# A two-layer graph network on one core: row factors of the first head broadcast by TensorE, maxima subtracted between the first steps, first pair of the second layer tile by tile

## The reference

```python
def _L0_gnn_ref(input_features, adj, W, b):
    A = (adj != 0).astype(input_features.dtype)
    hidden = input_features @ W + b
    deg = jnp.sum(A, axis=0)
    return A @ hidden / deg[:, None]

def _L1_gnn_ref(h, adj_mat, W, a):          # 4 heads of 512, SLOPE 0.01
    ht = (h @ W).reshape(N, N_HEADS, N_HIDDEN).transpose(1, 0, 2)
    src = jnp.einsum('hnd,hd->hn', ht, a_src)
    dst = jnp.einsum('hnd,hd->hn', ht, a_dst)
    e = jax.nn.leaky_relu(src[:, :, None] + dst[:, None, :], SLOPE) + adj_mat[None]
    att = jax.nn.softmax(e, axis=-1)
    h_prime = jnp.einsum('hij,hjd->hid', att, ht)
    return h_prime.mean(axis=0)
```

## Time and profile before

| | us |
|---|---|
| median of 3 runs | 2495.39 |
| lowest, highest | 2494.52, 2496.39 |
| the profiled execution | 2494.08 |
| its span | 2492.3 |
| PE busy in it | 2447.1 (98%) |
| DVE busy | 1866.4 (75%) |
| ACT busy | 1258.9 (51%) |
| POOL busy | 49.3 (2%) |

### The profile page before, as it was taken

How to read it: one execution, slowest core, us unless ns; L and a number is a source line. 1 busy time by engine, 2 the same in 40 slices (tenths; PEclk the granted TensorE clock), 3 DMA queues, 4 the chain that set the end, 5 groups by cost and what they waited for, 6 DMA issues and landing times.

```text
span 2492.3 us, 42728 instructions
## 1 busy us (share of the span) xinstructions
PE 2447.1 (98%) x12328; PEld 1198.3 (48%) x12328; DVE 1866.4 (75%) x2560; ACT 1258.9 (51%) x1883; POOL 49.3 (2%) x44
## 2 busy tenths in 40 slices
PE   6999999799999999999999999999999999999999
PEld 3544447344444444444444444444444444444787
DVE  7588767876688766877668776687766887667776
ACT  4545546744455444554445544455444554444554
POOL 0000000000000000000000000000000000000000
PEclk9999999899999999999999999999999999999999
DMA  4286646200030000300003000030000300001000
GB/s 148 69 290 195 227 156 217 82 5 5 25 97 34 4 4 25 97 34 4 4 25 97 34 4 4 25 97 34 4 4 25 97 34 2 2 13 49 26 1 9
DMA packets 74223, 144.21 MB, mean 58 GB/s; under 512 B 4489, under 2 KB 11915, under 8 KB 72970
## 3 DMA queue, kind: packets, MB, share of 16 engines
q1 hardware_dynamic: 74122, 143.08, 17.5%
HBM read 129.37 MB, written 13.70 MB: 57 GB/s over the span
## 4 chain that ended last, share of the span: by engine, by line
PE 94%; DVE 3%; DMA 1%; issue 1%; ACT 1%; SPq 0%; DVEq 0%; ACTq 0%
PE z_ps L731 70%; PE o_ps L759 11%; PE o_ps L1351 3%; PE z_ps L1351 3%; PE z_ps L1404 2%; PE c_ps L1322 1%; PE o_ps L1322 1%; DMA ring_reg<-adjT_in 1%; PE c_ps L1351 1%; DVE hl_reg L917 1%; PE c_ps L1383 1%; PE o_ps L1375 0%; PE o_ps L1309 0%; DMA h_reg<-x_in 0%; DVE w_reg L952 0%
## 5 line engine op out<-in xcount | busy, mean ns | idle before, releaser
L731 PE MATMUL z_ps<-hl_reg,h_reg 128*128 (+2 forms) x8736 | 1759.0, 364 | 11.1 <-DVE hl_reg L608 11.1
L731 PEld LDWEIGHTS z_ps<-hl_reg,h_reg 128*128 (+1 forms) x8736 | 855.2, 98 | 911.4 <-DVE hl_reg L608 11.4
L559 ACT ACTIVATE hl_reg<-t_reg (+2 forms) x364 | 361.9, 994 | 731.5 <-DVE t_reg L635 379.4
L608 DVE TENSOR_TENSOR hl_reg<-t_reg,hl_reg (+2 forms) x364 | 417.6, 1147 | 235.0 <-ACT hl_reg L559 233.3
L544 ACT ACTIVATE t_reg<-ring_reg,vv 128x512 f32 (+3 forms) x728 | 526.3, 770 | 66.0 <-DVE ao_reg L623 60.3
L635 DVE SCALAR_TENSOR_TENSOR t_reg<-t_reg,vv,e_reg (+3 forms) x728 | 510.3, 743 | 7.7 <-issue 7.7
L623 DVE TENSOR_TENSOR ao_reg<-ao_reg,t_reg 128x1024 f32<-128x1024 f32 (+1 forms) x336 | 383.7, 1142 | 0.0
L759 PE MATMUL o_ps<-w_reg,z_reg 128*128 128x512 f16 x1248 | 278.2, 379 | 0.9 <-DVE z_reg L651 0.9
L759 PEld LDWEIGHTS o_ps<-w_reg,z_reg 128*128 128x128 f16 x1248 | 119.8, 98 | 140.9 <-DVE z_reg L651 1.2
L651 DVE SCALAR_TENSOR_TENSOR z_reg<-z_ps,z_reg 128x512 f16<-128x512 f32 (+1 forms) x112 | 73.2, 653 | 151.6 <-ACT z_reg L571 151.6
L456 ACT ACTIVATE e_reg<-e_reg (+2 forms) x91 | 90.1, 996 | 152.0 <-DVE e_reg L467 151.9
(11 more groups left out here) (165 smaller groups left out, 1066.9 us busy)
## 6 DMA issues: line engine op xcount, KB each, us to landing
ring_reg<-adjT_in SPq DMA_DIRECT2D x78, 512.0 KB, 4.6
e_reg<-adjT_in SPq DMA_DIRECT2D x78, 512.0 KB, 3.6
ring_reg<-x_in SPq DMA_DIRECT2D x13, 512.0 KB, 4.2
x_dram<-ring_reg SPq DMA_DIRECT2D x13, 512.0 KB, 5.1
ring_reg<-c_dram SPq DMA_DIRECT2D x24, 256.0 KB, 3.3
ao_reg<-x_dram SPq DMA_DIRECT2D x6, 1024.0 KB, 5.6
out_dram<-ao_reg SPq DMA_DIRECT2D x6, 1024.0 KB, 4.4
h_reg<-x_in SPq DMA_DIRECT2D x3, 1536.0 KB, 16.7
```

Of the source, the lines that this page charges most:

```text
L559: nc.scalar.activation(hl_ring[:, g % HL_RING, 0, :, 0:W], t_ring[:, g % T_RING, :, 0:W], ACT.Copy).then_inc(hi_ready, 1)
L608: nc.vector.tensor_tensor(hl_ring[:, g % HL_RING, 1, :, 0:W], t_ring[:, g % T_RING, :, 0:W], hl_ring[:, g % HL_RING, 0, :, 0:W], ALU.subtr ...
L731: mm = nc.tensor.matmul(z_ps[:, k, 0:W], hk[hs], hl_ring[:, r, ps, u, 0:W], start=first and u == 0 and n == 0, stop=last and u == 1 and n ...
```

## The change

The work is the same but for where scales are applied; the order around the start of the second layer is another.

- **Scores read where they are.** The scaled copy of the scores (L1134) goes; the reduction and the two operations after it read the scores from PSUM, and the factor 1/HS moves into the scale of the exponentials. The exponentials of the column factors go to a buffer of their own (`ev`), from which two DVE operations make the three parts of `vv`; the mask of the last tile follows later, during the first step.
- **Row factors of the first head.** PE makes the broadcast rows itself, by four transpositions of a column of `rows_c` read 128 times over, into one bank; ACT copies the bank to `c_bc[:, 0]`. The rows of all heads are still transposed, copied (from a different buffer) and sent through DRAM, later, and only the heads 1 to 3 are loaded back for block 0.
- **Order on ACT and DVE.** The third early exponential stands behind that of the row factors. The subtractions of the pairs 3, 4 and 5 follow the steps 1, 2 and 3, that of pair 6 and both splits follow step 4; the exponentials of these pairs and the high halves accordingly on ACT.
- **First pair tile by tile.** For pair 0 of segment (0, 0) the high and the low half are made for each tile of 512 columns, and PE takes the first tile (12 matmuls over the four banks) when its low half is there, then the second.

```diff
@@ layer2_scalar(act, c_rows, high1)
                 if isinstance(p, int) and p == 0:
-                    act.wait_ge(c_in[h], (b + 1) * 16)
+                    if isinstance(b, int) and b == 0 and h == 0:
+                        act.wait_ge(c0_sb, 1)
+                        act.wait_ge(s_vvp, 2)
+                    else:
+                        act.wait_ge(c_in[h], (b + (h > 0)) * 16)
...
                 for p in range(2, LOOP0):
                     step(b, h, p)
+                    if isinstance(b, int) and b == 0 and h == 0:
+                        exp_e(act, 0, E_PRE0 + p - 1)
+                if isinstance(b, int) and b == 0 and h == 0:
+                    for j in range(LATE_SPLIT, PAIRS):
+                        high1(j)
...
             t1(0, 0, 0)
-            for p in range(2):
-                step(0, 0, p)
+            for u in range(2):
+                act.wait_ge(p_ready, u + 1)
+                nc.scalar.activation(hl_ring[:, 0, 0, u], t_ring[:, 0, u],
+                                     ACT.Copy).then_inc(f_hi if u == 0 else hi_ready, 1)
+            t1(0, 0, 1)
+            step(0, 0, 1)
+            exp_e(act, 0, E_PRE0)
+            c_rows()
@@ layer2_vector(dve, split1)
                 for p in range(4, LOOP0):
                     step(b, h, p)
+                    if isinstance(b, int) and b == 0 and h == 0:
+                        subtract_max(dve, 0, E_PRE - 1)
+                        for j in range(LATE_SPLIT, PAIRS):
+                            split1(j)
...
-            for p in range(4):
-                step(0, 0, p)
+            step(0, 0, 0)
+            for u in range(2):
+                if u == 0:
+                    dve.wait_ge(f_hi, 1)
+                else:
+                    dve.wait_ge(hi_ready, 1)
+                nc.vector.tensor_tensor(hl_ring[:, 0, 1, u], t_ring[:, 0, u], hl_ring[:, 0, 0, u],
+                                        ALU.subtract).then_inc(f_lo if u == 0 else lo_ready, 1)
+            last = vv[:].rearrange("p (r t) -> p r t", t=NT)[:, :, NT - 1]
+            nc.vector.tensor_scalar(last, last, valid[:, NT - 1:NT], None, ALU.mult).then_inc(s_vmask, 1)
+            accumulate(0, 0, 0)
+            for p in range(1, 4):
+                step(0, 0, p, before=(0, 0, p - 1) if p > 1 else None, lone=p == 1)
+                subtract_max(dve, 0, E_PRE0 + p - 1)
@@ layer2_tensor
-            pair(0, 0, 0, first=True)
+            for u in range(2):
+                if u == 0:
+                    pe.wait_ge(f_lo, 1)
+                else:
+                    pe.wait_ge(lo_ready, 1)
+                for k in range(KT):
+                    for n, (hs, ps) in enumerate(((0, 0), (0, 1), (1, 0))):
+                        mm = nc.tensor.matmul(z_ps[:, k], h16[:, u, hs, k * P:(k + 1) * P], hl_ring[:, 0, ps, u],
+                                              start=u == 0 and n == 0, stop=False)
+            mm.then_inc(hl_free, 1)
@@ sync
                 sp.wait_ge(cr_out, 16)
-                for h in range(H):
+                for h in range(1, H):
                     load_c(sp, 0, h)
@@ vector
                 dve.wait_ge(sd_ps, NT)
-                link(dve, nc.vector.tensor_scalar(sdc, c_ps[:, 0:NT * 2 * H], 1.0 / HS, None, ALU.mult))
-                nc.vector.tensor_reduce(dmx[:], sdc.rearrange("p (t r) -> p r t", r=2 * H), AX_X,
-                                        ALU.max).then_inc(s_dmx, 1)
+                nc.vector.tensor_reduce(dmx[:], sd_rt, AX_X, ALU.max).then_inc(s_dmx, 1)
...
                 dve.wait_ge(s_vv, 2)
...
-                for p in range(E_PRE0, E_PRE):
-                    subtract_max(dve, 0, p)
-                for j in range(LATE_SPLIT, PAIRS):
-                    split1(j)
-                layer2_vector(dve)
+                nc.vector.tensor_scalar(vv4[:, 2], ev4[:, 0], -PS, None, ALU.mult).then_inc(s_vvp, 1)
+                nc.vector.tensor_scalar(vv[:, 0:2 * H * NT], ev, PS, None, ALU.mult).then_inc(s_vvp, 1)
+                dve.wait_ge(s_vvp, 2)
+                layer2_vector(dve, split1)
@@ scalar
-                for p in range(E_PRE0):
+                for p in range(E_PRE0 - 1):
                     exp_e(act, 0, p)
...
+                nc.scalar.activation(cc3, cc3, ACT.Exp, scale=1.0 / HS).then_inc(s_cexp, 1)
+                exp_e(act, 0, E_PRE0 - 1)
+                act.wait_ge(cb_ps, 1)
+                act.wait_ge(x1_out[0], 16 * sum((NA + i) % ADJ_RING == 0 for i in range(PAIRS)))
+                nc.scalar.activation(c_bc[:, 0], o_ps[:, 1], ACT.Copy).then_inc(c0_sb, 1)
@@ tensor
                 pe.wait_ge(tr_sb, NT)
+                for t in range(IT):
+                    mm = nc.tensor.transpose(o_ps[:, 1, t * P:(t + 1) * P], rows_c[:, t:t + 1].broadcast_to((P, P)),
+                                             ident[:])
+                mm.then_inc(cb_ps, 1)
                 nc.tensor.transpose(o_ps[0:H * NT, 0, 0:P], rows_c[:], ident[:]).then_inc(cr_ps, 1)
```

## The result

Median of 20 runs: 2492.12 us, against 2495.34 for the kernel before (20 runs). The ratio is 0.9983, interval 0.9977 to 0.9989, which is 4.2 us less (2.7 to 5.7); the two medians differ by 3.2. The prediction was 2490.4 with a range of 2488.1 to 2493.2, and "within 0.2%" as the likeliest outcome, with 0.57.

A forecast was written before the change was run, and what follows sets the result against it. DVE's queue order was taken to bound PE's 11.1 us wait between the layers. An opening gain of 7.0 less a stall of 2.0 leaves 5.0 us: the median of 2495.39 becomes 2490.4, range 2488.1 to 2493.2.

The forecast's parts named there:

- The bound: Between the layers PE idles 11.1 us; DVE's queue order is the bound, the row factors through DRAM nearly as late.
- The opening: Start of the second layer: PE's first matmul moves from 458.39 to 451.36, a gain of 7.0 us.
- the reads of PSUM: Reduction and two operations after it on DVE: 0.05 us more each from PSUM, 0.15 in all (0 to 0.33).
- The steps up to the fifth: First segment: DVE's low halves 1 to 3 come 0.9, 1.3 and 2.0 us before PE wants them.
- S + 25.3: S is the end of the first tile's low half (451.31); low half 4 was to end 25.3 us later, at 476.6.
- The stall: Before the fifth pair PE waits 2.0 us for low half 4, leaving 5.0 of the 7.0 us gained.
- The loop: After the fifth step DVE's low halves follow every 5.18 us, PE's own pace; PE loses 0 to 0.3 us over six pairs.
- Rival (a): The clock falls in PE's stall of 2.0 us, costing 2.1 more: 2492.5; chance 0.15.
- (b): DVE gets through the fifth step in 7.2 us, so PE has no stall; gain 7.0, 2488.4; chance 0.11.
- (c): DVE's chain is slower than PE: POOL blocks the first accumulation (2.0) or the loop lengthens (1.8); 2492.3; chance 0.12.
- (d): Something no row shows holds the first activation at 453; opening gains 2.2, the stall takes 2.0; 2495.2; chance 0.04.
- (e): PE's short waits at each pair keep it at 1.2 GHz, 5.1 us a pair; no change or slower; chance 0.03.

The follow-up runs named there:

- dram_factors: Changed kernel with the first head's row factors sent through DRAM as before and no broadcast by PE: 2496.83 us, 0.9999 of the kernel before.
- old_order: Changed kernel with DVE's and ACT's old order, subtractions, splits, high halves and exponentials ahead of the first step: 2493.93 us, 0.9987 of the kernel before.
- high_first: Changed kernel with the two moved high halves on ACT ahead of the exponential of pair 6: 2487.98 us, 0.9963 of the kernel before.
- after_fourth: Changed kernel unaltered, run for a fourth profile: 2492.99 us in one run.

## Why the prediction was right, point by point

**The bound.** Read rightly for DVE, incompletely for ACT. I wrote that DVE's order is the bound and the row factors nearly as late. dram_factors shows that the factors alone hold PE to within 3.1 us of the old start, and old_order that with the broadcast in place ACT's queue, 5.7 us ahead of the first activation, is later than DVE's, which waits 1.10 us for it. What I had put down to the factors' way through DRAM, the activation at 453.22, was in the kernel before the end of ACT's queue. I never summed that queue.

**The opening: 7.0 predicted, 7.33 measured.** The chain came out piece by piece, 1.12 for the transpositions, 0.60 for the copy, the exponential (1.04) hidden beside them. The 0.3 come from the reads of PSUM, which I had priced at +0.15 in all. From the reduction to PE's transposition it is 2.32 us (449.12 - 446.80) where it was 2.62, so 0.45 less than my sum; 0.15 of it was lost again in the steps from the transpositions to PE's start (4.93 us for 4.78). The reduction took 0.37 (0.53 before) and the first of the two operations 0.27, against 0.34 before:

```profile
445.27 0.34 DVE L1139 TENSOR_TENSOR ao_reg<-ao_reg,dall 128x104 f32<-128x104 f32 x1 [0.53 <-POOL dall L892]
```

The range's lower end, no change, was wrong too: these reads are faster from PSUM here. The fixed costs of 58 and 120 cycles that the Trainium skill gives in "VectorE: DVE Perf Modes", in the section on the TRN2 errata, point the other way; for these operations of 104 and 208 columns the measurement decides.

**The steps up to the fifth: right.** Low halves 1 to 3 came before PE asked for them, in four profiles. The fifth pair started 25.49 us after the first, where I had S + 25.3 and PE's start 0.05 behind S. DVE's wait for the exponential and the first high half took 2.07 us, for 2.1.

**The stall: 2.0 predicted, 1.70 measured, 5.0 left predicted, 4.64 measured.** Here terms were mis-sized, and luck helped the sum. I took the time at which PE wants the fifth pair, 23.3 us after its start, from ACT's waits on the ring. These end some 0.2 us after PE's pairs (counted at 5.18 us a pair from the first projection back), and the third came 5.50 us after the second, which I read as a slow pair of PE; PE's pairs take 5.18. Counted back from the first projection (240 matmuls in 51.8 us) the fifth pair of before started 22.8 after the first. That is 0.5 of gain too much. With it 5.0 + 0.3 (opening) - 0.15 (25.49 for 25.34 from PE's start to the fifth pair) - 0.5 = 4.64: the errors partly cancel. The stall itself came out shorter only because the first pair took 8.25 instead of 7.4 us at the low clock. The prediction had said that this would be hidden, and it was. In other executions the stall was 3.0 and 3.1.

**The loop: the outcome right, the reason wrong.** I held 5.18 us for the pace of DVE and ACT between themselves. After the change DVE's low halves follow at 4.9 us, 478.00 to 482.90:

```profile
482.90 1.22 DVE L630 TENSOR_TENSOR hl_reg<-t_reg,hl_reg  x1
```

The 5.18 of the earlier trace rows were PE's own pace, handed back through the ring. So DVE regained 0.3 us of lead a pair, and PE had no second wait.

**From the sum to the median.** The profile's 4.6 us agree with the ratio (4.2, interval 2.7 to 5.7). The median of the first set moved by 3.2, to 2492.12 where I had 2490.4, and 0.4 of these 1.7 us are the sum's (4.64 for 5.0). Rival (a), the clock lost at the stall, had been given 0.15 as an alternative and is in truth a part of the executions: it came in one of four profiles of the changed kernel, for 1.7 us (2.1 had been predicted), which makes 0.4 on average. With 0.8 to either side of the forecast the text drew the two as exclusive; they are a mixture. The remaining 0.9 must, by the profiles, lie ahead of the last tile, where the prediction had no term: the clock fell there too, in three of the four profiles, and the only profile of before, from which I counted, shows no such fall. How often before's other executions have it, the record doesn't show. In the later sets the medians differ by 5.1 and 4.6, so the forecast of 5.0 was missed by 1.8, 0.1 and 0.4.

**The rivals.** (b), no stall, is what high_first makes real: at 90.30 to the projection it lies 6.8 us below before, where (b) said 7.0. (c) didn't happen: POOL's operation lay beside the first accumulation (L942 at 454.91), which took 0.68 us (0.69 before); POOL's operation itself took 0.55 here, not 2.03. (d) didn't happen. (e), a clock that stays low pair after pair, didn't: where the clock fell, it was back by the end of the same pair.

## What to carry to other kernels

When work is moved off the path before a stage into its first steps, sum the follower's queue to the step where its lead ends, waits on the other engine included: the end of that sum, not the new start, is what is gained, and whatever makes the bound engine faster before that point (an earlier clock, a finer first tile) is worth nothing or half. Then look at the order of single instructions at that step: here one exponential that nobody needed soon, ahead of two copies that DVE waited for, cost 2.15 us where 4.64 were left, and swapping them gives a better version by a few lines, high_first (0.9963, of which 1.2 us aren't shown to be its own). And before two profiles are compared, cut them at a point both pass: here 3.0 us of difference lay ahead of it, 1.6 of them a fall of the clock that some executions of a kernel have and others don't. Two wait times read from a ring that the bound engine drives show that engine's pace, not the pace of those who wait.

## What the runs showed of the hardware

- A stall of PE loses the granted clock in some executions and not in others, over the same range of lengths. At the fifth pair it was lost with stalls of 2.11, 3.04, 3.10 and 3.10 us and held with 1.70, 1.82, 2.45 and 3.02; at the wait of 1.96 to 1.97 us in the first layer it was lost in 4 of 14 profiles. Each of these falls cost 1.35 to 1.69 us in matmuls.
- The clock can fall after PE has resumed: 1.2 us after it in after_fourth, whose stall shows 1.00 to its end.
- Matmuls put into the waits kept the clock in one profile of three (eight of them in 1.89 us); in the other two it fell all the same (3.21 and 3.35 us), and they held up the work behind them.
- DVE reading 104 and 208 float32 columns with a stride was faster where that operand lay in PSUM than where it lay in SBUF: 0.27 against 0.34 us, and 0.37 against 0.53.
- How long the clock stays low after the start of a dense stretch varies between executions of the same program: 24 matmuls of 512 columns took 6.71 to 8.25 us there.
